# Writing the first rows and the expert scatters straight into the output tensor of a graph-attention and mixture-of-experts layer

## What is computed

```python
x = x + gnn(_layernorm(x), edge_index, W, b_w, a, b_a)       # [2500, 512], 40000 edges
xf = _layernorm(x)
probs = softmax(xf @ Wg + bg)                                # 8 experts
_, top_idx = jax.lax.top_k(probs, 2)
mask = any(top_idx[:, :, None] == arange(8), axis=1)
comb = probs * mask
for e in range(8):
    h = gelu(xf @ W1[e] + b1[e])                             # 512 -> 256
    y = h @ W2[e] + b2[e]                                    # 256 -> 512
    out = out + comb[:, e:e + 1] * y
x = x + out
```

## Time and profile before

| what | us |
|---|---|
| median of 3 runs | 864.01 |
| lowest and highest of them | 863.16, 866.09 |
| the profiled execution | 861.91 |
| its span, from first to last instruction | 860.2 |
| busy: PE, PEld, DVE, ACT, POOL | 635.0, 501.5, 465.4, 370.7, 449.6 |
| last scatter issued (line 608) | 836.40 |
| copies to the output issued (lines 487, 1094) | 841.37, 841.38 |
| KB of each copy | 2500.0 |

### The profile page before, as it was taken

The page is one execution under the profiler, slowest core; times in us unless marked ns, Lnnn a source line. Parts: engine busy times, 40 slices in busy tenths (PEclk is TensorE's granted clock), DMA queues, the critical chain, the costliest instruction groups (busy, mean ns, idle before and its releaser), DMA issues.

```text
span 860.2 us, 13772 instructions
## 1 busy us (share of the span) xinstructions
PE 635.0 (74%) x2956; PEld 501.5 (58%) x2957; DVE 465.4 (54%) x1165; ACT 370.7 (43%) x982; POOL 449.6 (52%) x533
## 2 busy tenths in 40 slices
PE   4999254766776666776676676958889999999960
PEld 3777243655555555665555565745547788888840
DVE  5998433555555555565555555789495433333320
ACT  4443332434433343444343443527763454545430
POOL 5000575666666666666666666410105677777750
PEclk9999777999899998889998998887998999999995
DMA  6243475666666666666666665507994477777767
GB/s 198 100 158 106 145 214 160 180 175 177 185 175 175 178 185 175 178 182 177 177 193 169 176 192 168 146 24 263 322 376 167 90 135 136 137 132 139 134 90 249
DMA packets 58300, 146.97 MB, mean 171 GB/s; under 512 B 8868, under 2 KB 18708, under 8 KB 57880
## 3 DMA queue, kind: packets, MB, share of 16 engines
q0 software_dynamic: 35216, 106.84, 49.3%
q1 hardware_dynamic: 22968, 37.16, 12.4%
q10 hardware_dynamic: 80, 2.56, 0.9%
HBM read 118.17 MB, written 33.47 MB: 176 GB/s over the span
## 4 chain that ended last, share of the span: by engine, by line
PE 37%; DVE 22%; issue 15%; another core or an unknown queue 9%; DVEq 7%; DMA 4%; POOLq 1%; ACT 1%; POOL 1%; SPq 0%; ACTq 0%
PE ps L711 17%; PE ps L850 6%; PE ps L864 4%; DVE S L1239 4%; DVE acc L1248 4%; DVE Wt L1227 3%; PE ps L665 3%; DMA result<-y,si 2%; PE ps L840 2%; DVEq L1279 1%; PE ps L791 1%; DVEq L1248 1%; PE ps L761 1%; DMA xg<-xn_table,gi 1%
## 5 line engine op out<-in xcount | busy, mean ns | idle before, releaser
L711 PE MATMUL ps<-rows,S 128*128 128x257 f32 x1252 | 322.4, 420 | 157.6 <-DVE acc L1248 124.6
L512 POOL DMA_INDIRECT rows<-node_table,srcT x313 | 296.2, 946 | 243.4 <-issue 84.1
L711 PEld LDWEIGHTS ps<-rows,S 128*128 128x128 f32 x1252 | 260.2, 212 | 219.6 <-issue 159.2
L958 ACT ACTIVATE E<-sdst_w,rows 128x128 f32 x313 | 100.1, 390 | 281.6 <-DVE Wt L1227 150.3
L1248 DVE TENSOR_TENSOR acc<-acc,ps 64x514 f32 x160 | 110.1, 688 | 155.2 <-remote 94.5
L1239 DVE SCALAR_TENSOR_TENSOR S<-ps,lane,Wt 128x128 f32<-128x128 f32 x313 | 88.2, 345 | 22.3 <-issue 14.1
L958 ACT ACTIVATE ps<-sdst_w,rows 128x128 f32 x313 | 96.0, 351 | 0.0
L850 PE MATMUL ps<-W_e,xgT 128*128 x352 | 83.4, 380 | 0.0
L608 POOL DMA_INDIRECT result<-y,si x44 | 70.4, 1601 | 11.3 <-issue 5.8
L850 PEld LDWEIGHTS ps<-W_e,xgT 128*128 128x128 f32 x352 | 63.4, 190 | 6.9
L665 PE MATMUL ps<-Wb,xT 128*128 128x512 f32 x240 | 59.1, 403 | 2.5 <-DVE dstT L1191 1.4
(11 more groups left out here) (209 smaller groups left out, 641.9 us busy)
## 6 DMA issues: line engine op xcount, KB each, us to landing
W_e<-in_L_ffn_W_dram SPq DMA_DIRECT2D x16, 512.0 KB, 9.2
node_table<-rows SPq DMA_DIRECT2D x20, 258.0 KB, 2.6
result<-acc SPq DMA_DIRECT2D x20, 256.0 KB, 2.5
xn_table<-xn SPq DMA_DIRECT2D x20, 256.0 KB, 2.2
rows<-node_table,srcT POOLq DMA_INDIRECT x313
x_all<-in_x_dram SPq DMA_DIRECT2D x19, 256.0 KB, 3.0
out_dram<-result SPq DMA_DIRECT2D x1, 2500.0 KB, 16.7
out_dram<-result ACTq DMA_DIRECT2D x1, 2500.0 KB, 18.4
```

The lines of the kernel that those rows point to most:

```text
L512: nc.gpsimd.indirect_dma_start(out=rows[:, g % RING, c, :], out_offset=None, in_=table, in_offset=bass.IndirectOffsetOnAxis(ap=srcT[:, GC ...
L711: m = pe.matmul(ps_agg[q][:, a, 0:HALF], S[:, w, c, :], rows[:, r, c, a * HALF:(a + 1) * HALF], start=(c == 0), stop=(c == n - 1))
L958: m = nc.scalar.activation(e[:, c, :], sdst_w[:, bass.ds(w, 1), :].rearrange("p w n -> p (w n)"), ACT.Exp, bias=bias, scale=scale)
```

## The change

The name `result` now stands for the output tensor itself, which the wrapper declares with 3072 rows instead of 2500. The stores of x1, the stores of the padding blocks and the scatters are written as before and go there. Both copies and `st_out` are gone. SP keeps its waits on the scatters and gets an increment of a new semaphore, a wait for the x1 stores and a wait for the increment. ACT ends after its last activation. The host takes the first 2500 rows of the array that comes back.

```diff
-    result = nc.dram_tensor("result", [NTN + YR * P, D], F32).ap()
+    result = out
+    assert result.shape[0] == NTN + YR * P
...
-        st_out = sem("st_out")
+        all_in = sem("all_in")
...
             for r in range(YR):
                 sp.wait_ge(put_y[r], 16 * n_rounds + 16)
-            sp.dma_start(out[0:N // 2, :], result[0:N // 2, :]).then_inc(st_out, 16)
-            sp.wait_ge(st_out, 32)
+            sp.sem_inc(all_in, 1)
+            sp.wait_ge(st_x1, 16 * NT)
+            sp.wait_ge(all_in, 1)
...
             share_of(4 * n_rounds - 1, YR - 1)
-            for r in range(YR):
-                act.wait_ge(put_y[r], 16 * n_rounds + 16)
-            act.dma_start(out[N // 2:N, :], result[N // 2:N, :]).then_inc(st_out, 16)
-            act.wait_ge(st_out, 32)
...
-    shape = _np.shape(inputs["x"])
-    args.append(nc.dram_tensor("out_0_dram", shape, _mybir.dt.float32, kind="ExternalOutput").ap())
+    n, d = _np.shape(inputs["x"])
+    rows_out = -(-n // P) * P + 4 * P
+    args.append(nc.dram_tensor("out_0_dram", (rows_out, d), _mybir.dt.float32, kind="ExternalOutput").ap())
...
-    return r.results[0]["out_0_dram"]
+    return r.results[0]["out_0_dram"][0:n]
```

## The result

| | median us | lowest to highest | runs |
|---|---|---|---|
| before | 863.59 | 861.05 to 866.09 | 4 |
| changed | 849.34 | 847.43 to 855.05 | 4 |

The ratio of the two is 0.9848, with a 95% interval of 0.9814 to 0.9883: the change saves 1.5%, between 10 and 16 us, and the medians are 14.25 us apart. The forecast had been 14.2 us less, at 849.8.

What follows compares the result with a forecast made beforehand. The end was taken as bound by four serial scatters, then the copies, then the closing. Old end 860.2 against new end 846.0 gives 14.2 us: 864.01 - 14.2 = 849.8 us, range 844.7 to 852.0.

Steps and rivals of the forecast that it cites:

- The stretch that goes: At the program's end, both copies and the wait behind them go, from 841.3 to 859.8: 18.5 us.
- What is late next: At the close, GpSimd's drain ends last at 845.8, plus 0.2 us release: end 846.0, gain 14.2 us, not 18.5.
- How sure the drain's end was: GpSimd's closing drain ends between the landing at 841.3 and 845.8; the upper end was taken, at 0.66.
- a fixed trail behind the last scatter: Reading of GpSimd's closing drain: its end work follows the last scatter by a set time, so 845.8 stands.
- a handling of finished transfers slowed by the copies: Other reading of GpSimd's closing drain: copies at 284 GB/s delay it, so without them it ends before 845.8.
- The argument that the drain had "already outlasted the engine's last instruction by 3.4 us": At the close: the drain was held 3.4 us before the copies began, so they can act only on the rest.
- First rival: At the close, GpSimd's drain shrinks with the copies: gain 18.5 us, 845.5 us; chance 0.15, partly shrunk 0.12.
- The rule of the Trainium skill: At the close, drains are about 12 ns constant on all five engines, so the gain would be 18.4 us.
- Second rival: In the last 25 us, scatters with addition land slower in the output; 72% growth eats the gain; much slower: 0.03.
- Third rival: At the close, something not on record holds the program as long: 864 us; no shortening or just eaten gain, 0.03.
- The stores of first rows: SP's 20 stores into the output, before ACT's `minus_i`, land by 619.6 and cost 0, with 2.9 us to spare.
- What the prediction said of the profile after: At the end: last scatter issued near 836.4, landed near 841.3; GpSimd drain some 9.6 us; releases at about 846.0.

Runs made afterwards that it cites:

- e3: The changed kernel with `result` again an internal table that is never copied to the output: 777.37 us, ratio 0.9840 to the kernel before.
- e2: The changed kernel with its block closed by semaphores alone, without GpSimd's closing drain: 775.09 us, ratio 0.9796 to the kernel before.
- e8: The changed kernel closed without GpSimd's drain, measured a second time in another group: 841.21 us, ratio 0.9802 to the kernel before.
- e5: The changed kernel with two GpSimd drains in a row after all gathers have been used: 843.55 us, ratio 0.9839 to the kernel before.
- e7: The kernel before, both full copies kept, closed without GpSimd's drain: 858.28 us against 859.22, ratio 1.000.
- e1: The changed kernel again, unaltered, as the measure for its group: 778.00 us against 790.71 for the kernel before, ratio 0.9824.
- e6: The kernel before with its two output copies cut to 160 rows each: 845.36 us, ratio 0.9845 to the uncut kernel before.
- e9: The changed kernel with two drains after the gathers and GpSimd waiting for the last landing before its closing drain: 777.81 us, ratio 0.9818 to the kernel before.
- e4: The changed kernel with GpSimd waiting for its last scatters to land before its closing drain: 778.61 us, ratio 0.9846 to the kernel before.

## Why the prediction was right

**The stretch that goes.** It was put at 18.5 us, from the last wait on a scatter to the end of the wait on the copies. The copies and that wait are gone from the profile after, and e3 shows that they and not the destination make the gain.

**What is late next.** This was the step that mattered, and it was right: the end is set by GpSimd's drain, not by SP. It was read off as ending 4.5 us behind the last landing, with 0.2 us for the release, and so measured (853.1 against 848.6, span 853.4). The gain of 14.2 us is the 18.5 us, less the 4.5 that the drain had kept hidden, with an end 0.2 us behind the drain where it was 0.4 behind the wait on the copies. Whoever takes the copies' 18.4 us from the page as the gain is too high by 4 us; e2 and e8 are what it takes to get them.

**How sure the drain's end was.** The two readings offered were a fixed trail behind the last scatter, and a handling of finished transfers slowed by the copies. The forecast took the first, and the number held. But the runs show that the reason was neither. The trail isn't fixed: it runs from 0.09 to 4.51 us with the transfers issued since the drain before. And it isn't slowed by traffic: it is 4.51 us beneath 284 GB/s of copies and 4.51 us with the DMA engines at 0 GB/s. It was the same on both sides, and the change leaves those 405 transfers as they are, in number, kind and order. The argument that the drain had "already outlasted the engine's last instruction by 3.4 us" before the copies began supported the right value for a poor reason: those 3.4 us are the wait for the landing, which every drain begun ahead of one shows here. The right choice between the two ends, to which the forecast gave 0.66, was in this part luck. That the medians came out within 0.5 us of the forecast is luck too, with an interval of 10 to 16 us for the gain; what bears the sum out is the trace, where the stretch from the last landing to the end of the span is 18.9 us before and 4.7 after, 14.2 less.

**First rival**, the drain shrinks with the copies: wrong, by the equal trails. **The rule of the Trainium skill**, about 12 ns for a drain at the end (VectorE: DVE Perf Modes, The DRAIN you can't avoid), is near the measured 13 ns for SP, and ACT's 8 ns, when they are idle. GpSimd comes nearest with nothing issued since the drain before, 40 ns (e5); with hundreds of its own transfers behind it, it is off by 9 us, of which 4.5 are exposed. The page speaks of drains that the runtime puts around a program, though, and the drain of line 60 belongs to the kernel's own block, since e2 and e7 leave it out by an argument of the block. So the runs say that the rule doesn't carry over to such a drain, not that it is wrong for the ones that it names.

**Second rival**, a slower target for additions: wrong. The landing times are alike to 0.04 us in the median, in both pairs, e3 and e1 as well as before and after. Growth by 72% would have been needed.

**Third rival**, a close that holds as long in another way: wrong; the time outside the span is 855.05 - 853.4 = 1.7 us, as before.

**The stores of first rows** were to cost 0, with 2.9 us to spare. They land in 2.5 us as a rule and 5.5 at most after the change, against 5.6. The last is in by 620.9 + 5.5 = 626.4 at the latest, and ACT needs them at 630.0, so that the cover stands, with 3.6 us to spare:

```profile
L459 SPq DMA_DIRECT2D out_dram<-acc x20: 562/582/1389, 584.6 to 620.9; - x20
...
DMA to landing us min/median/max: 2.5/2.5/5.5
```

```profile
L1075 ACT ACTIVATE minus_i<-ident x1: 293/293/293, 630.0 to 630.0; 128x128 fp32r<-128x128 f32 x1
```

**What the prediction said of the profile after** held in the stretches and not in the positions: the last scatter was to be issued near 836.4 and is at 844.1, for the 8.4 us lost before the expert stage in that execution. For the 6.8 us lost ahead of the first store to the output the destination is ruled out by the order; 4.9 of them lie between the last gather (551.1 and 553.0) and that store. The other 1.6 lie between it and the first `xg` gather, a stretch of 69.6 us before and 71.2 after. That stretch is 71.2 us in e6 and 69.8 in e7, with an internal table, and 71.1 in e5 and 69.5 in e8, with the output tensor, all four on one chip: both lengths come up with either destination. What the execution of 855.05 us lost them to stays open.

## What to carry to other kernels

When the last thing in a program is taken away, read which engine drains next and when: the gain is the distance to that, not the length of what is taken away. A closing GpSimd drain can lie hidden under a final copy, and its price then appears in full when the copy goes; where every transfer has a semaphore that some engine waits for anyway, a close by semaphores alone gave it back here (4 us), and where something longer covered it, it gave nothing (e7). A results table whose only reader is a copy to the output can be written as the output itself, padding rows included: here, additions by indirect DMA into the output tensor landed as fast as into an internal one.

## What the runs showed of the hardware

A GpSimd drain does more than wait for landings. With everything landed it took 4.06 us behind 313 indirect transfers (in e5 and again in e9), 4.64 behind 92 and 5.34 behind 405, and 0.040 us directly behind another drain. Begun ahead of the last landing, it ended 0.09, 0.30, 3.81 and 4.51 us behind it for 1, 6, 92 and 405 transfers: 41 to 42 ns each up to 92, then almost level (4.43 and 4.47 us for 399 and 404). Elapsed time and the kind of transfer are not parted from the number at the low end. The 313 stand out, since they took less than the 92 of e9; they were gathers only, and their last was issued 20 and 14 us earlier, and which of the two matters stays open.

The same program's time differs by nearly a tenth from chip to chip, 790.71 us against 863.59. The tensor engine's granted clock goes with it: 0.96 of full speed on average in the profiles of e1 to e4, 0.91 in the two of the first chip. The trail at the end, in which nothing is computed, is 4.51 us on both.
